# Attention-weighted context sum rebuilt from one-pass fp32r products of high and low parts

## The reference, cut to what matters

```python
x = x + xattn(layernorm(x), ctx_768, Wq, Wk, Wv, Wo, bo)   # x (128, 32, 256), ctx (128, 257, 192)
x = x + attn(layernorm(x), ln_g, ln_b, Wx, Ww, bw, Wk, Wv, Wr, Wo)
x = x + ffn(layernorm(x), U1, V1, b1, U2, V2, b2)

def xattn(x, context, Wq, Wk, Wv, Wo, bo):                  # 8 heads of 64
    q, k, v = x @ Wq, context @ Wk, context @ Wv            # split into heads
    attn = softmax(einsum('bhsd,bhld->bhsl', q, k) * 64 ** -0.5)
    return einsum('bhsl,bhld->bhsd', attn, v) @ Wo + bo
```

## Time and profile before

| | before |
|---|---|
| median of 3 runs | 1172.24 us (1168.86 to 1172.98) |
| the profiled execution | 1169.72 us, its span 1167.6 us |
| PE busy | 1113.0 us (95%) |
| DVE busy | 617.7 us (53%) |
| ACT busy | 578.7 us (50%) |
| POOL busy | 256.2 us (22%) |
| granted PE clock over the span | 0.983 of full |

### The profile page before, as it was taken

One profiled execution on the slowest core, in us unless ns is written; L12 is line 12 of the kernel. 1 busy time (PEld: TensorE's weight loads), 2 busy tenths in 40 slices (PEclk: granted clock), 3 DMA queues, 4 the chain that ended last, 5 costly groups with the idle time before them and its releaser, 6 DMA issues.

```text
span 1167.6 us, 18934 instructions
## 1 busy us (share of the span) xinstructions
PE 1113.0 (95%) x7052; PEld 776.1 (66%) x7052; DVE 617.7 (53%) x1256; ACT 578.7 (50%) x1374; POOL 256.2 (22%) x324
## 2 busy tenths in 40 slices
PE   4899999999999999999999999999999999998875
PEld 2557676766767677676767667676766767666653
DVE  2234656474655647465564646556464654646362
ACT  2445446354554645455463545546354554635121
POOL 0011304032130403213041321304132130414030
PEclk9999999999999999999999999999999999999887
DMA  7222221212222121222222122221212212120000
GB/s 262 91 75 73 75 73 59 83 49 67 65 67 82 58 83 49 67 65 67 83 58 82 50 67 64 67 83 58 80 51 67 64 59 83 49 82 25 10 3 15
DMA packets 57992, 79.06 MB, mean 68 GB/s; under 512 B 10288, under 2 KB 39728, under 8 KB 57904
## 3 DMA queue, kind: packets, MB, share of 16 engines
q1 hardware_dynamic: 54304, 72.71, 20.6%
q10 hardware_dynamic: 3600, 5.16, 1.2%
HBM read 73.38 MB, written 4.46 MB: 67 GB/s over the span
## 4 chain that ended last, share of the span: by engine, by line
PE 86%; DVE 5%; issue 4%; ACT 3%; POOL 2%; ACTq 1%; DVEq 0%; POOLq 0%
PE acc L357 9%; PE scores L334 9%; PE scores L337 7%; PE gb L423 7%; PE acc L359 6%; PE gb L309 5%; PE gb L395 5%; PE gb L446 5%; PE ptp L346 5%; PE gb L411 5%; PE gb L320 5%; PE gb L494 3%; PE gb L484 2%; PE gb L469 2%; PE gb L299 2%
## 5 line engine op out<-in xcount | busy, mean ns | idle before, releaser
L551 ACT ACTIVATE probs<-scores,nmax 128x257 f32<-128x257 f32 x256 | 119.4, 472 | 199.5 <-DVE nmax L682 199.4
L851 POOL TENSOR_TENSOR ptm<-probs,head 128x32 f32<-128x32 f32 x128 | 31.0, 242 | 657.6 <-DVE probs L689 657.6
L682 DVE TENSOR_REDUCE nmax<-scores 128x2 f32<-128x514 f32 x128 | 88.3, 690 | 156.2 <-PE scores L337 156.2
L741 DVE COPY_PREDICATED s<-mask,gb 128x256 f32<-128x256 uint8 x256 | 106.2, 442 | 89.9 <-PE gb L446 85.5
L357 PE MATMUL acc<-pt,raw_n 128*128 128x256 f32 x512 | 140.7, 397 | 0.0
L334 PE MATMUL scores<-raw_t,qk 128*128 128x257 f32 x512 | 132.6, 381 | 1.2 <-ACT qk L582 1.2
L561 ACT ACTIVATE pc<-acc 128x512 f32<-128x512 f32 x128 | 76.8, 600 | 112.4 <-PE acc L359 112.4
L357 PEld LDWEIGHTS acc<-pt,raw_n 128*128 128x128 f32 x512 | 89.9, 190 | 32.5 <-issue 22.3
L556 ACT ACTIVATE pt<-ptp 128x512 f32<-128x512 f32 x128 | 77.1, 602 | 51.7 <-PE ptp L346 50.1
L687 DVE RECIPROCAL rinv<-rsum 128x2 f32<-128x2 f32 x128 | 21.2, 166 | 144.0 <-ACT probs L551 143.9
L334 PEld LDWEIGHTS scores<-raw_t,qk 128*128 128x128 f32 x512 | 87.3, 190 | 8.5 <-issue 1.6
(11 more groups left out here) (101 smaller groups left out, 2112.8 us busy)
## 6 DMA issues: line engine op xcount, KB each, us to landing
raw_t<-in_ctx_t SPq DMA_DIRECT2D x128, 258.0 KB, 3.2
raw_n<-in_ctx_n SPq DMA_DIRECT2D x128, 192.0 KB, 2.4
xin<-in_x SPq DMA_DIRECT2D x16, 256.0 KB, 3.2
xb<-in_x SPq DMA_DIRECT2D x16, 256.0 KB, 2.9
vsp<-tail_values SPq DMA_DIRECT2D x256, 2.0 KB
out<-ob SPq DMA_DIRECT2D x16, 256.0 KB, 2.8
wq<-in_wq ACTq DMA_DIRECT2D x1, 512.0 KB, 4.8
wk<-in_wk SPq DMA_DIRECT2D x1, 512.0 KB, 6.2
```

The costliest lines, as they stand in the source:

```text
L551: go(probs[n % 2][:, r, 0:L], scores[:, r, 0:L], ACT.Exp, bias=nmax[:, r:r + 1], accum_out=rsum[:, r:r + 1]).then_inc(s["exp_ready"], 1)
L682: v_.tensor_reduce(nmax[:], scores[:, :, 0:L], AX.X, ALU.max, negate=True)\
L741: last = v_.copy_predicated(s2[:, first:first + 3:2], mask[:, l0 + l:l0 + l + 1].to_broadcast([P, 2, P]), t[:, :, l * P:(l + 1) * P])
```

## The change

PV no longer uses plain fp32 matmuls. Each factor is written as a high part, rounded to the type fp32r, and a low part, the rest, and PV is the sum of high times high, high times low and low times high, each an fp32r matmul:

- ACT copies `ptp` to `pth` (high, in place of `pt`), and copies the context batch `raw_n` to `nat` (high, 384 elements per partition) ahead of the exponentials (`n_hi`).
- DVE subtracts `pth` from `ptp` and gets `ptl` (`pt_lo`, 512 elements per partition), ahead of `nmaxs`.
- POOL subtracts `nat` from `raw_n` in two instructions of 256 and 128 elements (`n_lo`), ahead of `tail_column`.
- PE does ten fp32r matmuls of 256 columns with 128 weight columns in place of two fp32 matmuls with 128 and two with 64 weight columns. PV waits for DVE's `ptl` and POOL's `n_lo` where it waited for ACT's `pt` and the transfer.
- The rings of `raw_t` and `raw_n` have two buffers instead of three; the one of `raw_n` is free when `n_lo` has read it. `xt3` shares `xt1`, `xn2` shares `xn1`, `qf` shares `pf`, with no new wait.

```diff
--- before.py
+++ after.py
@@ -5,6 +5,7 @@
 import numpy as np
 
 F32 = mybir.dt.float32
+F32R = mybir.dt.float32r
 U8 = mybir.dt.uint8
 ACT = mybir.ActivationFunctionType
 ALU = mybir.AluOpType
@@ -25,7 +26,7 @@
 EPS = 1e-5
 A_MIN = 2.0 ** -25
 LEVELS = 4
-RING = 3
+RING = 2
 BANKS = 4
 
 
@@ -134,7 +135,9 @@
         raw_t = [sb(f"raw_t{i}", [P, 2, LP]) for i in range(RING)]
         raw_n = [sb(f"raw_n{i}", [P, LT, C]) for i in range(RING)]
         probs = [sb(f"probs{i}", [P, 2, LP]) for i in range(2)]
-        pt = sb("pt", [P, LT, 256])
+
+        nat = [sb(f"nat{i}", [P, LT, 2 * C], F32R) for i in range(2)]
+        pth, ptl = sb("pth", [P, LT, 256], F32R), sb("ptl", [P, LT, 256], F32R)
         nmax, rsum, rinv = sb("nmax", [P, 2]), sb("rsum", [P, 2]), sb("rinv", [P, 2])
         qk = [sb(f"qk{i}", [P, 2, G, 256]) for i in range(2)]
         pc = sb("pc", [P, 2, H, T])
@@ -144,6 +147,7 @@
 
 
         xin, xn0, xt1 = sb("xin", [P, 2, D]), sb("xn0", [P, 2, D]), sb("xt1", [P, 2, T])
+        xt3 = xt1
         qs = sb("qs", [P, 4, T])
         stats, mv = sb("stats", [P, 3, 2, 6]), sb("mv", [P, 3, 2, 2])
         ve, rstd, half = sb("ve", [P, 3, 2]), sb("rstd", [P, 3, 2]), sb("half", [P, 2])
@@ -160,8 +164,9 @@
 
 
         o2 = sb("o2", [P, 2, T])
-        xn2, xt3 = sb("xn2", [P, 2, D]), sb("xt3", [P, 2, T])
-        pf, qf = sb("pf", [P, T]), sb("qf", [P, T])
+        xn2 = xn1
+        pf = sb("pf", [P, T])
+        qf = pf
         hid = sb("hid", [P, 8, T])
         ob = sb("ob", [P, 2, D])
 
@@ -185,8 +190,8 @@
         ctxn_in = [sem(f"ctxn_in{i}") for i in range(RING)]
         bank_filled = [sem(f"bank_filled{i}") for i in range(BANKS)]
         bank_drained = [sem(f"bank_drained{i}") for i in range(BANKS)]
-        names = ("half_ready zeros_ready small_ready scores_ready nmax_ready exp_ready probs_ready pt_ready ptev_ready "
-                 "acc_ready pc_ready ptm_ready var0_ready var1_ready var2_ready rstd0_ready rstd1_ready rstd2_ready xn0_ready xn1_ready xn2_ready xb_ready ob_ready "
+        names = ("half_ready zeros_ready small_ready scores_ready nmax_ready exp_ready probs_ready pt_ready pth_ready ptl_ready "
+                 "nhi_ready nlo_ready acc_ready pc_ready ptm_ready var0_ready var1_ready var2_ready rstd0_ready rstd1_ready rstd2_ready xn0_ready xn1_ready xn2_ready xb_ready ob_ready "
                  "tanh_ready f_ready inv_ready pw_ready bdec_ready khat1_ready hat_ready dve_chain").split()
         s = {n: sem(n) for n in names}
 
@@ -215,7 +220,7 @@
 
             def load_n(n):
                 if n >= RING:
-                    sp.wait_ge(s["acc_ready"], 2 * (n - RING + 1))
+                    sp.wait_ge(s["nlo_ready"], n - RING + 1)
                 sp.dma_start(raw_n[n % RING][:], ctxn_v[n]).then_inc(ctxn_in[n % RING], 16)
 
             def load_x(g):
@@ -340,7 +345,7 @@
             def turn_probs(n):
                 pe.wait_ge(s["probs_ready"], n + 1)
                 if n > 0:
-                    pe.wait_ge(s["ptev_ready"], n)
+                    pe.wait_ge(s["ptl_ready"], n)
                 for r in range(2):
                     for t in range(LT):
                         last = nc.tensor.transpose(ptp[:, t, r * P:(r + 1) * P],
@@ -348,16 +353,18 @@
                 last.then_inc(s["pt_ready"], 1)
 
             def pv(n):
-                pe.wait_ge(s["ptev_ready"], n + 1)
-                pe.wait_ge(ctxn_in[n % RING], 16 * (n // RING + 1))
+                pe.wait_ge(s["ptl_ready"], n + 1)
+                pe.wait_ge(s["nlo_ready"], n + 1)
                 if n > 0:
                     pe.wait_ge(s["pc_ready"], n)
-                x = raw_n[n % RING]
+                x = nat[n % 2]
                 for t in range(LT):
-                    mm(acc[:, 0], x[:, t, 0:P], pt[:, t], start=t == 0, stop=t == 1)
+                    for k, (c0, p_) in enumerate(((0, pth), (0, ptl), (2 * P, pth))):
+                        mm(acc[:, 0], x[:, t, c0:c0 + P], p_[:, t], start=t == k == 0, stop=t == 1 and k == 2)
                 for t in range(LT):
-                    mm(acc[64 * t:64 * t + 64, 1], x[:, t, P:C], pt[:, t], start=True, stop=True)\
-                        .then_inc(s["acc_ready"], 1)
+                    for k, p_ in enumerate((pth, ptl)):
+                        last = mm(acc[:, 1], x[:, t, P:2 * P], p_[:, t], start=t == k == 0, stop=t == k == 1)
+                last.then_inc(s["acc_ready"], 1)
 
             def tail_values():
                 out_ = tile("VT", 0)
@@ -551,12 +558,18 @@
                     go(probs[n % 2][:, r, 0:L], scores[:, r, 0:L], ACT.Exp, bias=nmax[:, r:r + 1],
                        accum_out=rsum[:, r:r + 1]).then_inc(s["exp_ready"], 1)
 
-            def pt_out(n):
+            def pt_hi(n):
                 act.wait_ge(s["pt_ready"], n + 1)
-                go(pt[:], ptp[:], ACT.Copy).then_inc(s["ptev_ready"], 1)
+                go(pth[:], ptp[:], ACT.Copy).then_inc(s["pth_ready"], 1)
+
+            def n_hi(n):
+                act.wait_ge(ctxn_in[n % RING], 16 * (n // RING + 1))
+                if n > 1:
+                    act.wait_ge(s["acc_ready"], n - 1)
+                go(nat[n % 2][:, :, 0:C], raw_n[n % RING][:], ACT.Copy).then_inc(s["nhi_ready"], 1)
 
             def pc_out(n):
-                act.wait_ge(s["acc_ready"], 2 * n + 2)
+                act.wait_ge(s["acc_ready"], n + 1)
                 b = n % G
                 go(pc[:, :, :, b * S:(b + 1) * S], acc[:].rearrange("p c (h s) -> p c h s", h=H), ACT.Copy)\
                     .then_inc(s["pc_ready"], 1)
@@ -626,8 +639,9 @@
                     if i == 1 and b == 0:
                         act.wait_ge(s["small_ready"], 1)
                     if 0 <= n < B:
-                        pt_out(n)
+                        pt_hi(n)
                     if 0 <= n + 1 < B:
+                        n_hi(n + 1)
                         exps(n + 1)
                     for name, g in before:
                         step(name, g)
@@ -681,6 +695,10 @@
                 dve.wait_ge(s["scores_ready"], 2 * n + 2)
                 v_.tensor_reduce(nmax[:], scores[:, :, 0:L], AX.X, ALU.max, negate=True)\
                     .then_inc(s["nmax_ready"], 1)
+
+            def pt_lo(n):
+                dve.wait_ge(s["pth_ready"], n + 1)
+                v_.tensor_tensor(ptl[:], ptp[:], pth[:].bitcast(F32), ALU.subtract).then_inc(s["ptl_ready"], 1)
 
             def norm_probs(n):
                 dve.wait_ge(s["exp_ready"], 2 * n + 2)
@@ -827,6 +845,8 @@
                 for b in range(G):
                     n = i * G + b
                     gap(i, b, 0)
+                    if 0 <= n < B:
+                        pt_lo(n)
                     if 0 <= n + 1 < B:
                         nmaxs(n + 1)
                     gap(i, b, 1)
@@ -851,6 +871,13 @@
                 p_.tensor_tensor(ptm[g % 2][:, :, :, b],
                                  probs[n % 2][:, :, L - 1:L].rearrange("p r (o u) -> p r o u", o=1)
                                  .to_broadcast([P, 2, 2, H]), head[:], ALU.mult).then_inc(s["ptm_ready"], 1)
+
+            def n_lo(n):
+                pool.wait_ge(s["nhi_ready"], n + 1)
+                x, raw = nat[n % 2], raw_n[n % RING]
+                p_.tensor_tensor(x[:, :, 2 * P:3 * P], raw[:, :, 0:P], x[:, :, 0:P].bitcast(F32), ALU.subtract)
+                p_.tensor_tensor(x[:, :, C:2 * P], raw[:, :, P:C], x[:, :, P:C].bitcast(F32), ALU.subtract)\
+                    .then_inc(s["nlo_ready"], 1)
 
             def hat(n, g):
                 l = int(n[1])
@@ -916,6 +943,8 @@
                     n = i * G + b
                     part(i, b, 0)
                     if 0 <= n + 1 < B:
+                        n_lo(n + 1)
+                    if 0 <= n + 1 < B:
                         tail_column(n + 1)
                     part(i, b, 1)
 
```

## The result

| | before | after |
|---|---|---|
| median (8 runs each, same chip) | 1170.39 us (1166.48 to 1173.49) | 1181.12 us (1175.34 to 1183.64) |
| the profiled execution, its span | 1169.72 us, 1167.6 us | 1180.82 us, 1178.7 us |
| granted PE clock over the span | 0.983 | 0.977 |

The ratio is 1.0088, with an interval of 1.0065 to 1.0111: slower, by about 11 us or 0.9%. The time lies inside the range on record and inside the likeliest case's own range of 1160 to 1184, but not within 0.5% of before, where that case had its centre.

The account below looks back on a forecast made before the run. Bound: PE, and for 24 of 68 us a group an equally long DVE, POOL and ACT chain. Chain +2.0, PE -1.8, net +0.2 in 15 groups, +3; first group gains 3.0: 1172 us, range 1140 to 1214.

Parts of the forecast that it names:

- With 0.107, PV is 1.07: PE's PV: ten fp32r records at 0.107 us each, plus 0.1 per tiling change, saving 1.8 us a group.
- I take 0.8: Round 6: POOL's `n_lo` colliding with DVE's `xn0` and `b2` adds 0.8 us a group, bounds 0 to 1.2.
- the two terms of 0.1 for round 4: Round 4: 0.1 us for a late `pt_lo` and 0.1 for `n_lo` meeting `xn2`, per group.
- of which 0.2 is slack: Second chain: of the 2.2 us added per group, 0.2 is absorbed by spare time, leaving 2.0.
- the sum had +2.0 - 1.8 = +0.2: Per group: second chain grows 2.0 us net of slack, PE's part gives back 1.8; net +0.2, in 15 groups +3.
- The first group ... gains the full 3.0: First group, without recurrence or feed-forward work: all eight PVs' saving counts, 3.0 us.
- Rings ... Nothing.: Rings of two buffers and shared tiles: loads still come ahead of need, so no cost.
- (a): Likeliest rival: near a tie as summed, centred on 1172 us, 1160 to 1184 by the collisions' cost; chance 0.42.
- (b): Rival: clearly faster, second chain gives way and `pt_lo` hides; in full 48 us less, 1124, half 1148; chance 0.23.
- (c): Rival: slower, weight loads pace PV's ten matmuls; 1194 us at 0.134 a matmul, 1231 at 0.19; chance 0.15.
- (d): Rival: slower, an fp32r record in PV costs 0.213 us; 88 us more, 1260; chance 0.10.
- (e): Rival: slower, PE stalls in rounds 0 and 7 waiting for DVE or ACT; 1 us a group, 1188; chance 0.10.

Follow-up runs that it names:

- experiment 1: Changed kernel without DVE's `pt_lo`, the low part of the probabilities a constant zero: 1156.97 us, ratio 0.9894.
- experiment 2: Changed kernel without POOL's `n_lo`, the low part of the context a constant zero: 1169.38 us, ratio 0.9991.
- experiment 6: Changed kernel with five useless plain fp32 matmuls ahead of PV in round 6 of the second group alone: 1175.65 us, ratio 1.0052.
- experiment 12: Kernel before the change with rings of two context buffers and nothing else changed: 1261.15 us, ratio 1.0777.
- experiment 11: Changed kernel with rings of three context buffers instead of two: 1177.13 us, ratio 1.0041.
- experiment 10: Changed kernel, full computation, with first layer norm moved, maxima ahead of `pt_lo`, and `n_lo` of round 6 later: 1136.82 us, ratio 0.9704.
- experiment 5: Changed kernel with PV of rounds 1 to 3 replaced by ten matmuls of other sizes, to price a record: one execution, 1177.28 us.

## Why the prediction was right or wrong

**Right: the mechanism.** Two chains of nearly one length, PE gaining what the other one takes away. The chain leaves PE and returns at L501 as described, PE waits for `hid` and for `ptl`, maxima and `xn0` are late, and the experiments take each piece out and get its price back. The two `pt_lo` cost 1.20 (experiment 1), as in the sum. That a chain and PE's part add up to the group, each with its own price, is what the table of the two parts shows. What failed are two terms of the sum, a record of PV taken at 0.107 and a second group priced like any other, which had no term for the clock. `n_hi` takes 0.51 and `n_lo` 0.73 + 0.45, as priced.

**Wrong: "With 0.107, PV is 1.07".** The record is 0.118. In the five rounds that count, 50 records × 0.011 is 0.55 a group, some 8 us over 15 groups. From its first record to the next matmul PV took 1.39 in rounds 7 and 0 (forecast 1.28) and 1.47, 1.36 and 1.29 in rounds 1, 2 and 3 (forecast 1.18): 6.90 in all, where the forecast was 6.1 and before had the 7.9 of the sum. The 0.25 beyond the records lies where PV meets its neighbours and was not looked into. PE's part of the group, from L501 to the next group's maxima, shrank by 1.34 (44.45 to 43.11), of which the PVs gave 1.00 and the matmuls beside them 0.34, and not by 1.8. This is the largest term of the miss in the steady groups. The lower end of the bounds was taken as if it were reachable exactly; the row of L446, a record each 0.11, was used only as a limit on the weights. By the Trainium skill ("FP8 and Floating Point Precision", section TensorE Precision Notes) true fp32 takes four passes through the array. An estimate from that is a quarter of the time for one pass; measured, it is 0.118 against two records of 0.213, a ratio of 3.6.

**Too high: "I take 0.8" for the collision.** All that `n_lo` does costs 0.68 (experiment 2), and the three DVE instructions of round 6 grew by 0.67, so the 0.8 and the two terms of 0.1 for round 4 came to 0.68 beside the two `pt_lo`: 1.88 was added where 2.2 was forecast.

**Wrong: "of which 0.2 is slack".** It was read from the 0.14 us between the last Gelu (608.28) and L494 (608.42) in the next group. But the same 0.13 stands at 540.09 to 540.22, where the chain was called tight, and 0.13 in the changed kernel (546.46 to 546.59), where PE idles for 2.64: it is a part of the chain and no slack. Without either low part the stretch takes 23.72, before it took 23.75. The 1.88 came out as 1.86, against a forecast of 2.0. The group read closely was also an odd one: 68.35, where the other middle groups had 68.20, with the whole difference in the stretch of the chain and PE's part the same. Why that one was longer is open.

So the steady group, in the prediction's own terms, is +1.86 - 1.34 = +0.52, where the sum had +2.0 - 1.8 = +0.2. The dear record (0.46 with what goes with it) outweighs the chain's error of 0.14 the other way; over the 12 middle groups it is 6.3 us in place of some 2.4.

**Missing: the second group.** "The first group ... gains the full 3.0" looks about right (2.1 at the start and 0.2 more), but the second group was priced as any other. It cost 4.3, and by experiment 6 3.75 of that is the clock. The 2.1 at the start is not all PV's either: the kernel before ran at a granted clock of 0.51 from 33 to 36 us, the changed one at 1.00 in the same stretch, and how much of the 2.1 that makes was not measured. The prediction has no term for a wait that loses the clock, and this is the largest single part of the 11 us outside the steady groups.

**Right for the steady groups, for a reason that was too brief: "Rings ... Nothing."** Rings of two alone would have cost 8% (experiment 12). In the changed kernel they cost nothing in the steady groups, by the queues because the wait moved to `n_lo`; at the start they may account for some 4 of the 11 us (experiment 11). The prediction names the new release point, but treats it as incidental; it is the condition on which the rings rest.

**The rivals.** (a) is where the time landed, but its top doesn't follow from its terms: "if both collisions cost their most, 15 × 0.6 = 9 more" gives 1181, and the range says 1184. The measured 1181.12 got there by other terms, the record and the clock, while the collisions cost less than forecast. That it lies in (a) is luck. (b) is refuted as stated: `pt_lo` doesn't hide in rounds 5 and 6. Of its 48 us less, experiment 10 gets 33, once the second chain is out of the way. (c), "begins to decide at 0.12", was nearer than it looked: the pace is 0.118, but by streaming, not by weight loads (experiment 5). (d) and (e) are refuted, since records are 0.118 apart and PE is never idle in its part of the middle groups, which holds round 0 and all of round 7 from L501 on.

**The exclusion of DVE and POOL.** By the Trainium skill ("SBUF — State Buffer", section Who interferes with whom) `pt_lo`, with one input in PSUM, should stay undisturbed by POOL. The trace agrees: 675 to 693 ns in all 128 cases, while `b2`, with both inputs in SBUF, reaches 1303, and POOL's `n_lo` itself 1168 for a usual 727.

## What to carry to other kernels

When work moves from the bounding engine to others, look for the stretch in which a chain through the others is already as long as that engine's work: what is added there comes out at full price, however idle those engines are on average, and moving three items to other places turned this change from 0.9% slower into 3.0% faster (of which the layer norm's move gives the kernel before 0.2% as well). Before a gap between two engines is called slack, look whether it is there in every hand-over between them. A price taken from the ideal end of a bound deserves a term of its own in the range, when it is multiplied by 1280 matmuls. Before shrinking a ring, read what stands behind its wait in the queue, and not only how soon the data is needed.

## What the runs showed of the hardware

- fp32r matmuls of 256 columns start 0.116 to 0.118 us apart, those of 128 columns with 64 weight columns 0.060 apart, and those of 128 columns with 128 weight columns 0.111 apart. Why it is not 0.107, a quarter of two plain records, no run explains: the step is there with 64 weight columns too.
- After a stretch in which PE was busy for 1.85 of 4 us, the granted clock was 0.50 for about 10 us. In the kernel before PE was busy for 2.18 of the 4 us from 128 to 132 and kept full clock. What set the two stretches apart was left open.
- One small transfer costs its queue 0.5 to 0.7 us to issue; 16 of them are a wait of 9.5 us for whatever stands behind.
